# Float32 projections cut into four 32-column matmuls, with a new order for the maxima

## The reference

```python
xn = layernorm(x)
q, k, v = xn @ Wq, ctx @ Wk, ctx @ Wv              # 16 heads of 8; ctx has 1601 rows per batch
att = softmax(q @ k.T * 0.125)                      # per batch and head: 256 x 1601
x = x + tanh(g_xattn) * ((att @ v) @ Wo.T)
xn2 = layernorm(x)
logits = xn2 @ router_w.T                           # 8 experts, the best two per token
x = x + tanh(g_ffn) * sum_e cw[e] * (gelu(xn2 @ w1[e].T + b1[e]) @ w2[e].T + b2[e])
```

## Time and profile before

| | |
|---|---|
| time before, median of 3 runs | 1344.58 us (1342.93 to 1349.27) |
| the profiled execution: span | 1360.3 us |
| busy TensorE / VectorE / ScalarE / GpSimd | 1289.7 / 1157.6 / 1094.7 / 546.7 us |
| weight loads of TensorE | 627.0 us, beside its matmuls |
| mean granted clock of TensorE | 0.975 |

### The profile page before, as it was taken

The page is one execution under the profiler, slowest core; times in us unless marked ns, Lnnn a source line. Parts: engine busy times, 40 slices in busy tenths (PEclk is TensorE's granted clock), DMA queues, the critical chain, the costliest instruction groups (busy, mean ns, idle before and its releaser), DMA issues.

```text
span 1360.3 us, 38009 instructions
## 1 busy us (share of the span) xinstructions
PE 1289.7 (95%) x14041; PEld 627.0 (46%) x14041; DVE 1157.6 (85%) x2268; ACT 1094.7 (80%) x2190; POOL 546.7 (40%) x1208
## 2 busy tenths in 40 slices
PE   4899999999999999999999999999999999998992
PEld 2243444444444444444444444444444433497882
DVE  7897999999999999999999999999999999355334
ACT  1487898988889888898989898888989888864561
POOL 3231426262626262535353444444453512145441
PEclk7698999999999999999999999999999999999997
DMA  3232121212121212121222222222211110386886
GB/s 91 76 86 82 45 67 51 70 47 75 46 78 42 83 35 66 52 64 54 64 59 60 63 58 66 58 64 58 67 52 39 49 40 6 98 258 196 252 262 231
DMA packets 61077, 112.67 MB, mean 83 GB/s; under 512 B 13052, under 2 KB 36476, under 8 KB 60748
## 3 DMA queue, kind: packets, MB, share of 16 engines
q1 hardware_dynamic: 54043, 97.67, 24.6%
q0 software_dynamic: 4320, 8.99, 2.0%
q10 hardware_dynamic: 2529, 3.58, 0.8%
HBM read 52.77 MB, written 13.71 MB: 49 GB/s over the span
## 4 chain that ended last, share of the span: by engine, by line
PE 75%; DVE 16%; SPq 3%; issue 3%; DMA 1%; ACT 1%; POOL 0%; POOLq 0%; ACTq 0%; DVEq 0%
PE pv L821 27%; PE st L772 14%; PE mxp L794 13%; DVE mx L1546 13%; PE st L1038 5%; PE mxp L1048 4%; PE st L879 4%; PE st L888 2%; SPq L401 2%; PE st L900 1%; PE st L851 1%; PE st L923 1%; PE st L863 1%; PE st L933 1%; DVE x_sb L1741 1%
## 5 line engine op out<-in xcount | busy, mean ns | idle before, releaser
L1546 DVE TENSOR_REDUCE mx<-mxp 128x2 f32<-128x804 f32 x1024 | 985.2, 987 | 71.1 <-PE mxp L794 60.8
L1077 ACT ACTIVATE arena<-st 128x512 f32<-128x512 f32 (+1 forms) x1664 | 892.2, 595 | 88.8 <-PE st L772 82.2
L821 PE MATMUL pv<-arena 128*32 128x256 f32 x6656 | 535.6, 394 | 0.5 <-ACT pv_sb L1084 0.4
L794 PE MATMUL mxp<-kpack,qpack 48*128 48x402 bf16 x2048 | 457.0, 344 | 16.2 <-DVE mx L1546 14.8
L772 PE MATMUL st<-qpack,kpack 51*128 51x256 bf16 (+1 forms) x3328 | 449.2, 273 | 2.4 <-DMA qpack<-mxT 2.1
L772 PEld LDWEIGHTS st<-qpack,kpack 51*128 51x128 bf16 (+1 forms) x3328 | 199.4, 97 | 202.4 <-ACT arena L1077 108.0
L794 PEld LDWEIGHTS mxp<-kpack,qpack 48*128 48x128 bf16 x2048 | 142.6, 93 | 167.0 <-DVE mx L1546 94.3
L821 PEld LDWEIGHTS pv<-arena 128*32 128x32 f32 x6656 | 131.6, 108 | 177.0 <-issue 89.3
L659 POOL CAST mxs<-nmx 128x8 bf16<-128x8 f32 x64 | 12.4, 193 | 263.3 <-DVE nmx L1554 263.2
L1218 ACT ACTIVATE arena<-st,bias 128x256 f32<-128x256 f32 (+1 forms) x172 | 74.1, 438 | 54.7 <-PE st L1038 38.4
L702 POOL DMA_INDIRECT results<-ysb,idx x71 | 68.9, 971 | 89.2 <-DVE ysb L1683 58.2
(11 more groups left out here) (194 smaller groups left out, 908.7 us busy)
## 6 DMA issues: line engine op xcount, KB each, us to landing
kpack<-ksp SPq DMA_DIRECT2D x750, 50.0 KB
arena<-in_w12T SPq DMA_DIRECT2D x43, 576.0 KB
arena<-in_ctxT SPq DMA_DIRECT2D x15, 800.5 KB, 4.5
qpack<-qsp SPq DMA_DIRECT2D x187, 32.0 KB
xblk<-rows SPq DMA_DIRECT2D x28, 132.0 KB
rows<-in_pads SPq DMA_DIRECT2D x8, 264.0 KB
arena<-results SPq DMA_DIRECT2D x8, 256.0 KB, 6.9
arena<-results ACTq DMA_DIRECT2D x8, 256.0 KB, 7.2
```

Source lines behind the costliest of these rows:

```text
L794: eng.matmul(mxp[pair % MX_BUFS][:, rg, 0:WIN], qpack[rows, b % 2, g * JJ + jj, t * P:(t + 1) * P], kpack[rows, b % 2, g * JJ + jj, WSTART ...
L821: ins = eng.matmul(pv[32 * j:32 * j + 32, 0:N], vaug[0:n, b % 2, kt, at:at + 32], pt[0:n, (2 * u + rg) % PT_BUFS, jj * N:(jj + 1) * N], st ...
L1077: eng.activation(pt[0:n, c % PT_BUFS, :], ring[bank_of["S", u, p]][0:n, :], ACT.Exp, scale=SCALE).then_inc(s_exp, 1)
L1546: eng.tensor_reduce(mx[:, tj, w, :], mxp[windows_done % MX_BUFS][:, :, 0:WIN], AX.X, ALU.max).then_inc(s_red, 1)
```

## The change

Six helpers of TensorE's program call `strips` in place of one `eng.matmul`. It cuts the 128 weight columns into four strips of 32, so that one matmul becomes four on the column tiles that the weighted values use, over the same moving columns and into the same PSUM bank. The tables of where the maxima, the keys of the first batch, the router logits and the small steps stand are replaced, and `FIRST` goes from 24 to 22.

```diff
+STRIP = 32
-TURN_AT, PLACE_AT = {8: 1, 22: 2, 34: 3, 47: 4}, {9: 1, 23: 2, 35: 3, 48: 4}
-POST_AT = {7: "C", 9: "F", 21: "L", 23: "R"}
-X_AT, Q_AT = 39, 43
-FIRST_K_AT = {7: 0, 9: 1, 10: 2, 11: 3}
+TURN_AT, PLACE_AT = {8: 1, 22: 2, 34: 3, 47: 4}, {8: 1, 23: 2, 35: 3, 50: 4}
+POST_AT = {7: "C", 9: "F", 21: "L", 22: "R"}
+X_AT, Q_AT = 41, 43
+FIRST_K_AT = {6: 0, 9: 1, 11: 2, 12: 3}
-L_NORM_AT, X_NORM_AT = 10, 26
-LOGITS_AT, EXP_AT, ROUTE_AT = 24, 26, 27
+L_NORM_AT, X_NORM_AT = 10, 21
+LOGITS_AT, EXP_AT, ROUTE_AT = 24, 25, 26
-FIRST, LEAD = 24, 30
-WINDOWS_AT = ("1011011110111111111111101001101110011111110111100111",
-              "1101111020000000000001101211100011100000011000120000")
-FIRST_WINDOWS_AT = ("1000000000000000000000000000000000000000000000000000",
-                    "1121121121222112111121121222111211211212111211121110")
+FIRST, LEAD = 22, 30
+WINDOWS_AT = ("1010011110110010111111101001100110020111011211100111",
+              "1111111020011010000000201211110011010001000000120000")
+FIRST_WINDOWS_AT = ("0002000001000011000000010000000100100000010101000000",
+                    "1121121212121102111122011222101111211211110200122110")
+            def strips(dst, weights, moving, **flags):
+                m = weights.shape[1]
+                for c in range(0, m, STRIP):
+                    n = min(STRIP, m - c)
+                    ins = eng.matmul(dst[c:c + n, :], weights[:, c:c + n], moving,
+                                     tile_position=(0, c), **flags)
+                return ins
-                eng.matmul(dst[:, 0:kn], wk_sb[:, :], ctx_sb[:, b % 2, k0:k0 + kn],
-                           start=True, stop=True).then_inc(s_kp, 1)
+                strips(dst[:, 0:kn], wk_sb[:, :], ctx_sb[:, b % 2, k0:k0 + kn],
+                       start=True, stop=True).then_inc(s_kp, 1)
```

More of the change, by code:

```diff
@@ L98 @@
 HEADS_AT = {2: 0, 42: 1}
-TURN_AT, PLACE_AT = {8: 1, 22: 2, 34: 3, 47: 4}, {9: 1, 23: 2, 35: 3, 48: 4}
-POST_AT = {7: "C", 9: "F", 21: "L", 23: "R"}
-X_AT, Q_AT = 39, 43
-FIRST_K_AT = {7: 0, 9: 1, 10: 2, 11: 3}
+TURN_AT, PLACE_AT = {8: 1, 22: 2, 34: 3, 47: 4}, {8: 1, 23: 2, 35: 3, 50: 4}
+POST_AT = {7: "C", 9: "F", 21: "L", 22: "R"}
+X_AT, Q_AT = 41, 43
+FIRST_K_AT = {6: 0, 9: 1, 11: 2, 12: 3}
 RANK_AT, LAST_RANK_AT, COUNT_AT, PLAN_AT = 46, 35, 38, 40
-L_NORM_AT, X_NORM_AT = 10, 26
-LOGITS_AT, EXP_AT, ROUTE_AT = 24, 26, 27
+L_NORM_AT, X_NORM_AT = 10, 21
+LOGITS_AT, EXP_AT, ROUTE_AT = 24, 25, 26
 ROWS_AT, LAST_ROWS_AT = {1: 40, 2: 42, 3: 44}, {9: 0, 10: 1, 11: 2, 12: 3}
-FIRST, LEAD = 24, 30
-WINDOWS_AT = ("1011011110111111111111101001101110011111110111100111",
-              "1101111020000000000001101211100011100000011000120000")
-FIRST_WINDOWS_AT = ("1000000000000000000000000000000000000000000000000000",
-                    "1121121212221112111121121222111211211212111211121110")
+FIRST, LEAD = 22, 30
[3 more added lines that the diff above has]
+                    "1121121212121102111122011222101111211211110200122110")
 PER_BATCH = NG * NMX
@@ L862, in queries @@
                 eng.wait_ge(s_xnT, b + 1)
-                eng.matmul(dst[:, 0:N], wq_sb[:, :], xnT[:, :], start=True, stop=True
-                           ).then_inc(s_qp, 1)
+                strips(dst[:, 0:N], wq_sb[:, :], xnT[:, :], start=True, stop=True).then_inc(s_qp, 1)
             def keys(b, c):
@@ L887, in values @@
                     n = key_rows(t0 + t)
-                    ins = eng.matmul(ring[i][0:n, t * D:(t + 1) * D],
-                                     ctx_sb[:, b % 2, (t0 + t) * P:(t0 + t) * P + n],
-                                     wv_sb[:, :], start=True, stop=True)
+                    ins = strips(ring[i][0:n, t * D:(t + 1) * D],
+                                 ctx_sb[:, b % 2, (t0 + t) * P:(t0 + t) * P + n],
+                                 wv_sb[:, :], start=True, stop=True)
                     if t == tn - 1:
@@ L922, in project @@
                 for t in range(NT):
-                    ins = eng.matmul(ring[i][:, t * P:(t + 1) * P], concT[:, t * P:(t + 1) * P],
-                                     wo_sb[:, :], start=True, stop=True)
+                    ins = strips(ring[i][:, t * P:(t + 1) * P], concT[:, t * P:(t + 1) * P],
+                                 wo_sb[:, :], start=True, stop=True)
                 ins.then_inc(s_f3p, 1)
@@ L932, in route @@
                 for t in range(NT):
-                    ins = eng.matmul(ring[i][:, t * NE:(t + 1) * NE], xn2T[:, t * P:(t + 1) * P],
-                                     rw_sb[:, :], start=True, stop=True)
+                    ins = strips(ring[i][:, t * NE:(t + 1) * NE], xn2T[:, t * P:(t + 1) * P],
+                                 rw_sb[:, :], start=True, stop=True)
                 ins.then_inc(s_rp, 1)
@@ L945, in rank_tokens @@
                 dst = ring[i][:, 0:NT * NE]
-                eng.matmul(dst, tri_bf[:, :], mask[:, :, :].rearrange("p t e -> p (t e)"), start=True, stop=False)
-                eng.matmul(dst, ones_bf[:, :], before[:, :, :].rearrange("p t e -> p (t e)"), start=False,
-                           stop=True).then_inc(s_rk, 1)
+                strips(dst, tri_bf[:, :], mask[:, :, :].rearrange("p t e -> p (t e)"), start=True, stop=False)
+                strips(dst, ones_bf[:, :], before[:, :, :].rearrange("p t e -> p (t e)"), start=False,
+                       stop=True).then_inc(s_rk, 1)
                 freed[i] = s_rkc, b + 1
```

## The result

The changed kernel takes 1323.95 us (median of 4 runs, 1319.23 to 1327.49), against 1345.68 us for the kernel before, run beside it (1342.93 to 1349.27). The ratio is 0.9844, with a 95% interval of 0.981 to 0.9878: 21.7 us, 1.6% faster. The profiled execution has a span of 1325.7 us.

A forecast was written before the change was run, and what follows sets the result against it. TensorE was taken to set the pace, with VectorE nearly full. A batch falls from 70.63 to 68.8 us: 25.9 us over fourteen periods, plus 1.8 in the first batch, gives 27.7 and 1317 us, range 1304 to 1333.

The forecast's parts named there:

- rival 3: Strip matmuls: four strips' shared reads of moving columns are served in turns; at double time about 1406 us; chance 0.05.
- rival 2: Strip matmuls: the array empties before them all the same, only the first batch gains 1 or 2 us: 1343; chance 0.04.
- rival 1: Batch period: VectorE takes over, waits grow to 3.3 us or more, 69.9 us a batch, 1333 us; chance 0.13.
- The terms of the 68.8 us before: TensorE's own work in one batch before the change, summed over units, second pairs, keys, values and small pieces.
- One of my signs of being wrong: Waits between maxima and their matmuls: forecast wrong if VectorE's go down but TensorE's go up by the same.
- the placing chain: First batch: SyncE's unbroken issues from placing the second group's maxima to the fourth's, to start 1.5 us earlier.
- the scores' wait: First batch: scores wait for SyncE to place the fourth group's maxima; 2.31 us before, to grow to 3 to 5.
- What I put at 0 for the end of the kernel: Last batch and experts: 0.4 us saved, three tile changes at 0.1 to 0.2 us lost, together 0.

The follow-up runs named there:

- strips apart: Changed kernel with the strips of keys and values moved from behind the weighted values to behind the unit's last maxima: ratio 1.0069 to the kernel before.
- The halved reductions: VectorE's maxima reductions read 201 of 402 columns: period 67.94 us in the changed kernel, 69.59 us in the kernel before.
- loads_last: Changed kernel, first batch's SyncE queue: third key group's packs moved to unit 35, loads of rows and context to unit 51: 1318.91 us, ratio 0.9812 to before.

## Why the prediction was right

**What a strip costs: right.** The step from the earlier trace rows, that a piece behind weighted values costs 1.68 ns a column and saves 0.20 us whatever its length, holds for keys (0.67 measured and forecast), queries (0.43 and 0.43), projection (0.44 and 0.43) and full values chunks (0.87 and 0.86). What reaches the batch is 0.15 to 0.22 us each. For the short values chunk it is only 0.05 of the 0.20 forecast, since the maxima behind it then wait for VectorE. That four strips read the same moving columns costs nothing: rival 3 is out. The instruction count is no limit either, with 32 records in 0.87 us. Strips of 64 columns and strips apart show that the cause is the change of tiles, so rival 2 is out.

**Logits and ranks: too cautious on their cost, right on what reaches the batch.** Logits cost 0.20 where I took 0.30, ranks 0.04 where I took no change: 0.10 and 0.11 us of TensorE's own work more than forecast. After the waits behind them logits save 0.22 us, where I took 0.24, and ranks nothing, as I took. By the 60 cycles of overhead per matmul in the Trainium skill's TensorEngine Tiling (Array Packing), section Performance Considerations, logits would have been 0.40, an estimate. Measured are 16 records in 0.20 us, 12 ns each, which is half of that. For these matmuls on four different tiles the trace doesn't agree with that rule.

**The period: right, with two errors that cancel.** Forecast 68.8, measured 68.88 us. TensorE's work fell by 2.45 and not 2.24 us; waits grew to 2.5 and not 2.2, well short of rival 1's 3.3. (The terms of the 68.8 us before add up to 68.6 if they aren't rounded first, so the waits before and after are known to some 0.2 us.) Fourteen periods give 24.5 us against 25.9. One of my signs of being wrong did come true. I expected both waits between the maxima and their matmuls to grow, but VectorE's fell by 1.8 us and TensorE's rose by 1.6. So it isn't two engines that wait for each other alike, but mostly TensorE that waits. I put the waits down to this pair. The halved reductions show 0.9 of the 2.5 us to be VectorE's, and the wait behind the ranks is ScalarE's; for the rest the cause is open.

**The first batch: the size right, the reason half wrong.** I expected the loop 1.8 us earlier, and the placing chain 1.5 us. The first scores start at 42.91 us instead of 45.87, 3.0 earlier. 1.2 of that stand already at the first turning of the maxima (39.76 for 40.92), ahead of which both kernels have the same 18 pairs; from there to the first scores it is 3.15 us for 4.95, the 1.8 of the forecast. The chain's first placing came 2.6 us earlier. Then, I wrote, what strips save would go into the scores' wait, which would grow to 3 to 5 us. The changed kernel's load of these scores:
```profile
104.98 0.21 PEld L782 LDWEIGHTS st<-qpack,kpack 51*128 51x128 bf16 x4 [1.92 <-DMA qpack<-mxT]
```
It waited for 1.92 us instead of 2.31. TensorE didn't get there early, for it waits for VectorE in the first batch (22.6 us from 40 to 130, before 25.8), which has 94 pairs to do either way. That SyncE's queue holds the place, that the `PLACE_AT` edits change nothing in its order, and that the wait and the half clock come together was right. The run loads_last shows the last, and so do two kernels whose queue is that of the changed kernel. Tables alone and strips for keys and values alone wait less at this place, and in both the granted clock is 1.00 from 60 to 130 us:
```profile
106.72 0.20 PEld L772 LDWEIGHTS st<-qpack,kpack 51*128 51x128 bf16 x4 [1.45 <-DMA qpack<-mxT]
```
```profile
104.72 0.20 PEld L782 LDWEIGHTS st<-qpack,kpack 51*128 51x128 bf16 x4 [1.28 <-DMA qpack<-mxT]
```
In the seven profiles that wait longer at this place, 1.92 to 4.07 us, a half-clock stretch follows.

**The total.** 27.7 us forecast, 21.7 measured (1317 and 1323.95 us), inside the range of 1304 to 1333. The attention, up to the last turning of heads, ends at 1158.7 us instead of 1185.1 in the two profiles: 26.4 us. What the medians lack against that, some 5 us, isn't found. There is no profile of the kernel before from an experiment in which it ran at 1344 us, so I can't say whether its experts' part is shorter there than the changed kernel's 166 us. The granted clock of each run, averaged over the whole of it, shows that half-clock time isn't the missing part. Beside the second profile of the changed kernel, the kernel before took 1343.1 to 1344.5 us at 0.979 and 0.980 and 1350.6 at 0.973; the changed kernel took 1321.9 and 1322.5 us at 0.979 and 1328.9 at 0.973. At equal clocks they are some 22 us apart and not 26. What I put at 0 for the end of the kernel can't be told from the differences in the experts' part either. The step that was too bold is to take a gain from one profiled execution off the median in full.

## What to carry to other kernels

Matmuls that stand next to column-tiled ones can use the same tiles, even if they fill all 128 columns: here it saved 0.15 to 0.22 us for each piece, but only 0.05 for a short one with 65 weight columns and nothing for two matmuls of 16 columns. The same strips between matmuls of other tiles cost 0.24 us a piece more. Count changes of tiles in TensorE's order, not the width of the matmuls.

Check what a shorter piece brings by the distance between two like groups around it, not by its own row in the chain. The ranks' row lost 0.11 us and their unit nothing, since the scores behind had to wait for a bank anyway.

When a wait comes from a queue that is busy without a pause, moving one batch of its issues moves the wait. List everybody who waits for that batch (here the placing, then ScalarE), and find the order that meets all of them.

## What the hardware showed that I had not expected

- Short matmuls on four column tiles run at some 12 ns for each record in their own row (16 in 0.20 us). The ranks' eight bfloat16 matmuls of 16 columns take 0.04 us there.
- In the changed kernel a wait of 2 us at one place in the first batch went with a half-clock stretch of 10 to 14 us behind it. In the two kernels that waited 1.28 and 1.45 us there, and in the order without waits longer than 0.8 us, that stretch was absent.
- The experts' part takes some 8 us more in some experiments than in others, whatever the kernel, at a DMA share near 0.8 in both cases. The cause is open.
